# Attention: head pairs taken one by one, and taken by twos, on TensorE

## The chip, the cores and the metric

The kernel runs on one core of a Trainium2 chip. The core has five engines that run their own instruction streams and meet only at semaphores: TensorE (PE, matmuls; its weight loads are listed as PEld), VectorE (DVE), ScalarE (ACT), GpSimd (POOL) and SyncE (SP, which here only issues transfers). The metric is the device time of one execution in microseconds (us). Of the kernel before there are three timed runs, 787.14, 789.05 and 790.76 us, median 789.05.

## The reference, cut to what matters

Tokens `x` (8 sequences of 256 tokens, 256 wide) go through two layers: a mixture of experts twice, then attention and a third mixture of experts. Only the attention is touched by the change:

```python
xn = layernorm(x, g_in)
q = (xn @ Wq).reshape(b, n, H, DH).transpose(0, 2, 1, 3) * scale   # H = 16 heads of DH = 64
k, v = split(xn @ Wkv)                       # one key and one value head for all 16
k, v = concat([null_k, k]), concat([null_v, v])                    # one more key and value
sim = q @ k.T + bias ; sim = causal and padding masks applied
attn = softmax(sim)
out = (attn @ v) -> (b, n, H * DH) ; out = layernorm(out @ Wo, g_out)
```

## The kernel before, in words

**Units of work.** The 8 sequences are batches `b` = 0 to 7. The 16 heads of a batch are taken as 8 pairs, so there are 64 pairs `p = 8 b + j`. The two heads of a pair lie in partitions 0 to 63 and 64 to 127; the 256 queries are two tiles of 128 (`i`), the second of which sees all 256 keys and the null key, the first only 129 columns.

**The path of a pair.**
1. TensorE projects the queries (`pe_queries`, L1516, two fp32 matmuls of 256 columns, each of which runs as two instructions of the trace) into PSUM bank `psY`. ScalarE copies them, scaled, to `c_qr` (`act_queries`, L1764), a ring of two.
2. TensorE makes the scores (`pe_scores`, L1530, four matmuls on 64 rows of the array, two heads at a time) in `psH` or `psHT`.
3. VectorE adds bias and mask and takes the row minimum (`dve_scores`, L1907), once for each head (`ORDER[0]`, `ORDER[1]`). ScalarE takes the exponentials with their sums (`act_exp`, L1770).
4. VectorE turns the weights in 32x32 blocks (`dve_blocks`, L1932, once for each head), takes the reciprocals of the sums (`dve_sums`, L1914) and turns those too (`dve_recs`, L1921).
5. SyncE stores the pair's blocks (512 KB) in memory (`sp_store_blocks`, L2406) and loads them back in another order (`sp_load_blocks`, L2417). The turned blocks on chip (`c_x1`) are a ring of two: the blocks of pair p overwrite those of p - 2, so `dve_blocks` waits until the store of p - 2 has landed.
6. TensorE sums weights times values (`pe_sum`, L1543, four matmuls with 64 output partitions each) in PSUM bank `psL`. VectorE multiplies by the reciprocals into `c_oT` (`dve_o`, L1941). TensorE multiplies by the output weights and accumulates over the batch's pairs in `psM` (`pe_out`, L1554).

**The order by hand.** Each engine's stream is written out: at its step p, TensorE does scores(p + 1), sum(p - 4), queries(p + 3) and out(p - 5). VectorE does blocks(p, first head), scores(p + 1, first head), O(p - 4) (that is `dve_o`), blocks(p, second head), reciprocals(p), scores(p + 1, second head). Work that comes once per batch is placed at chosen steps j of the batch: on VectorE the row statistics of the next batch and part of the routing of an earlier one at j = 1, routing at j = 3, the batch's output, routing and output statistics at j = 5, routing at j = 7; on TensorE the turned rows, keys and values of the next batch (L1565, L1571, L1578) and three small pieces of routing (L1592, L1600, L1613). Each engine runs its stream in order, so an instruction that waits holds all that stand behind it on its engine.

## Time and profile before

| | |
|---|---|
| the profiled execution's own time | 789.7 us |
| its span | 788.0 us |
| TensorE busy | 706.1 us, 90% |
| VectorE busy | 453.5 us, 58% |
| ScalarE busy | 371.1 us, 47% |
| GpSimd busy | 431.0 us, 55% |
| mean TensorE clock granted | 0.954 |
| L1932 (blocks turned) idle before it, while a store lands | 10.0 us of 15.1 |
| L1516, L1554 (queries, outputs), each 256 instructions | 71.8 and 67.8 us |

The pairs' loop runs from about 375 to 645 us of the span. The shares above are means over stages with different limits; the loop is read from its own stretch. In a timeline row the columns are start, length, engine, line, operation, output and inputs, the count of instructions merged in the row, and in square brackets the idle time of the engine ahead of it with what ended it. A matmul's end is modelled, so of neighbouring matmuls the distance of their starts is the better measure. In a row of stretches the columns are start:end, length, then busy time and instruction count of PE, PEld, DVE, ACT and POOL, then the granted clock (1.00 is 2.4 GHz, 0.50 is 1.2 GHz), the busy share of the DMA engines and GB/s.

### The profile page before, as it was taken

The numbers are of one execution on the slowest core, as the hardware profiler recorded it, in microseconds if no ns is written. First come the engines' busy times: TensorE is split into PE (matmuls) and PEld (weight loads), VectorE is DVE, ScalarE is ACT, GpSimd is POOL, SyncE is SP. The second block draws the span as 40 slices with busy tenths as digits, with TensorE's granted clock in tenths as the row PEclk, the third lists the DMA queues.
The fourth block names the chain that finished last, engine by engine and source line by source line (L and its number), as shares of the span: only waits on it lengthen the run. The fifth ranks groups of instructions, "written<-read, shape, count | busy, mean of one in ns | idle before, by whom it ended". The sixth has DMA issues, their size and how long they took to land. (4 is left out here: it accounts for less than half of the span.)

```text
span 788.0 us, 15682 instructions
## 1 busy us (share of the span) xinstructions
PE 706.1 (90%) x4459; PEld 550.4 (70%) x4460; DVE 453.5 (58%) x1695; ACT 371.1 (47%) x1096; POOL 431.0 (55%) x540
## 2 busy tenths in 40 slices
PE   8859997875899999998799999899999998988886
PEld 5348984564799999986466666576666654787775
DVE  1803456358223322323988989799998945345546
ACT  3535641224222222223766766566766535666611
POOL 1175406541555575243876877898897645255550
PEclk9988999785899999999999999899999999999998
DMA  9734634332799877611899999887888883445428
GB/s 324 289 107 121 159 107 126 101 117 64 247 347 322 301 247 273 209 44 52 293 302 340 324 329 336 278 300 240 306 272 292 261 280 135 123 139 150 143 85 309
DMA packets 100571, 173.28 MB, mean 220 GB/s; under 512 B 11152, under 2 KB 73744, under 8 KB 99472
## 3 DMA queue, kind: packets, MB, share of 16 engines
q1 hardware_dynamic: 78064, 115.32, 43.5%
q0 software_dynamic: 10944, 30.03, 11.9%
q10 hardware_dynamic: 11488, 27.04, 10.3%
q8 instruction: 34, 0.56, 0.3%
q14 instruction: 41, 0.34, 0.1%
HBM read 111.73 MB, written 60.62 MB: 219 GB/s over the span
## 5 line engine op out<-in xcount | busy, mean ns | idle before, releaser
L1770 ACT ACTIVATE work<-work 128x129 f32<-128x129 f32 (+1 forms) x256 | 114.4, 448 | 76.1 <-DVE work L1907 74.5
L1932 DVE STREAM_TRANSPOSE region_bd<-work 128x384 f32<-128x384 f32 x128 | 73.2, 572 | 15.1 <-DMA c_blocks<-region_bd 10.0
L1409 POOL DMA_INDIRECT d_pairs<-work,home x47 | 48.1, 1022 | 51.5 <-DVE home_f L1161 36.4
L1516 PE MATMUL psY<-work,region_ac 128*128 128x256 f32 x256 | 71.8, 404 | 3.8 <-ACT work L1764 3.8
L2228 POOL TENSOR_TENSOR work<-region_bd,region_ac 128x386 f32<-128x386 f32 x64 | 59.7, 939 | 21.1 <-DVE work L1907 14.0
L2228 POOL TENSOR_TENSOR work<-work,region_ac 128x386 f32<-128x386 f32 x64 | 59.6, 943 | 20.8 <-DVE work L1907 15.0
L1398 POOL DMA_INDIRECT b_pairs<-work,home x39 | 38.0, 974 | 59.7 <-DVE work L1105 57.7
L1554 PE MATMUL psM<-region_ac,work 128*128 128x256 f32 x256 | 67.8, 388 | 0.0
L1390 POOL DMA_INDIRECT work<-in_x,inv x39 | 37.1, 951 | 53.8 <-DVE inv L1318 32.8
L1079 ACT ACTIVATE work<-work 128x512 f32<-128x512 f32 x39 | 24.6, 631 | 86.1 <-DVE work L1098 61.6
L1543 PE MATMUL psL<-region_bd,work 128*64 128x256 f32 (+1 forms) x512 | 56.4, 341 | 7.9 <-DMA region_bd<-c_blocks 4.1
L887 PE MATMUL psH<-work,region_bd 128*128 128x128 f32 x472 | 59.9, 282 | 3.0 <-issue 1.8
L887 PEld LDWEIGHTS psH<-work,region_bd 128*128 128x128 f32 x472 | 57.3, 198 | 4.0 <-issue 2.5
L1543 PEld LDWEIGHTS psL<-region_bd,work 128*64 128x64 f32 x512 | 32.0, 137 | 39.3 <-issue 23.1
L1468 POOL DMA_INDIRECT work<-a_slots,slot_u x32 | 31.5, 985 | 46.2 <-DMA a_slots<-work 27.3
L1516 PEld LDWEIGHTS psY<-work,region_ac 128*128 128x128 f32 x256 | 45.7, 194 | 14.5 <-ACT work L1764 5.8
L1390 POOL DMA_INDIRECT work<-y_scratch,inv x39 | 37.6, 965 | 33.1 <-DVE inv L1318 21.6
L1554 PEld LDWEIGHTS psM<-region_ac,work 128*128 128x128 f32 x256 | 47.7, 192 | 8.8 <-issue 2.8
L1770 ACT ACTIVATION_READ_ACCUMULATOR work<-work 128x1 f32 x256 | 47.9, 187 | 0.0
L1907 DVE CUSTOM_DVE_ANT_0 work<-psH,work 128x129 f32<-128x129 f32 (+1 forms) x128 | 39.6, 346 | 13.4 <-issue 10.9
L947 PE MATMUL psH<-work,region_bd 128*128 128x128 f32 x320 | 41.2, 285 | 0.0
L2309 POOL DMA_INDIRECT d_rows<-region_bd x32 | 32.2, 1005 | 15.7 <-issue 6.6
(390 smaller groups left out, 1614.0 us busy)
## 6 DMA issues: line engine op xcount, KB each, us to landing
c_blocks<-region_bd SPq DMA_DIRECT2D x64, 512.0 KB
region_bd<-c_blocks SPq DMA_DIRECT2D x64, 512.0 KB
region_bd<-in_b_w ACTq DMA_DIRECT2D x37, 512.0 KB
work<-d_rows SPq DMA_DIRECT2D x47, 132.0 KB
a_slots<-work SPq DMA_DIRECT2D x19, 256.0 KB
region_bd<-in_b_w SPq DMA_DIRECT2D x1, 4096.0 KB, 15.1
work<-b_pairs ACTq DMA_DIRECT2D x12, 256.0 KB
region_bd<-in_d_w SPq DMA_DIRECT2D x12, 256.0 KB
```

The source lines that it names most:

```text
L887: last = pe.matmul(pair_h[p % DEEP][:, t % PAIR, j, :], f.w_in(j, k, t), xT[:, p % DEEP, t % PAIR, k, :], start=(k == 0), stop=(k == KD - 1))
L947: last = pe.matmul(ffn_h[u % RING][:, j * P:(j + 1) * P], f.w_in(j, k, u % RING), b_xT[:, u % 2, k, :], start=(k == 0), stop=(k == KD - 1))
L1390: pool.indirect_dma_start(out=slot_rows(f, t), out_offset=None, in_=st.src, in_offset=bass.IndirectOffsetOnAxis(ap=inv[:, t:t + 1], axis=0 ...
L1398: pool.indirect_dma_start(out=st.pair_dram, out_offset=bass.IndirectOffsetOnAxis(ap=home[:, t:t + 1], axis=0), in_=ys[:, t % RING, :], in_ ...
L1409: pool.indirect_dma_start(out=st.pair_dram, out_offset=bass.IndirectOffsetOnAxis(ap=home[:, t:t + 1], axis=0), in_=d_ys[:, t % ROWS, :], i ...
L1516: last = pe.matmul(psY[:, 0:SEQ], c_wq[:, c, j * P:(j + 1) * P], c_xnT[:, odd, c, :], start=(c == 0), stop=(c == KD - 1))
L1543: last = pe.matmul(psL[DH * o:DH * o + DH, queries].rearrange("p (i a q) -> p i a q", a=4, q=32), c_v[:, b % 2, n, :], weights[:, o, block ...
L1554: last = pe.matmul(psM[:, i * DIM:(i + 1) * DIM], c_oT[:, p % 3, i * P:(i + 1) * P], c_wo[:, j, :], start=(j == 0 and i == 0), stop=(j == ...
L1770: nc.scalar.activation(c_p[:, j % 2, o, a:z], c_sc[:, o, a:z], ACT.Exp, scale=-1.0, bias=c_min[:, o, i:i + 1], accum_out=c_sum[:, j % 2, o ...
L1907: last = nc.vector.tensor_tensor_reduce(c_sc[:, o, a:z], psS[j % 2][:, o, a:z], c_bm[:, 2 * (j % 2) + o, a:z], 1.0, -LOWEST, ALU.add, ALU. ...
L1932: nc.vector.transpose(out=c_x1[:, p % 2, :, (QT + 1) * o:(QT + 1) * (o + 1), :].rearrange("p b i q -> p i b q"), in_=c_p[:, j % 2, o, 1:1 ...
L2228: pool.tensor_tensor(c_bm[:, 2 * (j % 2) + o, :], c_mp[b % 2], c_bias[:, 2 * j + o, :], ALU.subtract).then_inc(C.bm_ready, 1)
```

## The change

TensorE takes the pairs by twos. Its round for the even pair a is scores(a + 2) and scores(a + 3), sum(a - 4) and sum(a - 3), queries(a + 4) and queries(a + 5), out(a - 4) and out(a - 3). The queries of two pairs fill both halves of `psY`, and ScalarE copies both in one instruction, ahead of its exponentials at even steps. The sums of two pairs lie interleaved in `psL` (tile i, then pair, then 128 columns); one VectorE instruction of 512 columns multiplies both (`dve_o(p - 6)`, at even steps p, which does pairs p - 6 and p - 5). `c_oT` holds two pairs where it held three. On VectorE the reciprocals of an even pair move to the next, odd step, behind that step's first blocks, so their store is issued there. SyncE issues two stores, then two loads, then up to two weight loads. The small pieces of routing and of the next batch move to other places of TensorE's and ScalarE's streams.

```diff
 def pe_queries(pe, k, j, odd, b):
-            wait(pe, C.qr_ready, k)
+            wait(pe, C.qr_ready, k if k < 2 else k - k % 2)
-                last = pe.matmul(psY[:, 0:SEQ], c_wq[:, c, j * P:(j + 1) * P], c_xnT[:, odd, c, :],
+                last = pe.matmul(psY[:, (k % 2) * SEQ:(k % 2 + 1) * SEQ], c_wq[:, c, j * P:(j + 1) * P], c_xnT[:, odd, c, :],
...
 def pe_sum(pe, p, j, b):
-            wait(pe, C.o_ready, p)
+            wait(pe, C.o_ready, p - p % 2)
+            sums = psL[:, :].rearrange("p (i r a q) -> p i r a q", i=QT, r=2, q=32)[:, :, p % 2, :, :]
...
 def pe_batch(pe, b, odd, first, last):
+            for k in range(NPAIR // 2):
+                a = NPAIR * b + 2 * k
+                x = a - LAG
+                for p in (a + 2, a + 3):
+                    if p < pairs:
+                        pe_scores(pe, p, p % NPAIR, p // NPAIR)
+                for s in (x, x + 1):
+                    if s >= 0:
+                        pe_sum(pe, s, s % NPAIR, s // NPAIR)
+                if k == 0 and b >= 2:
+                    pe_z_turn(pe, b - 2)
+                if k == 1 and not first and not last:
+                    pe_rows(pe, b + 1)
...
+                if k == 3 and not last:
+                    pe_v_turn(pe, b + 1)
+                for p in (a + 4, a + 5):
+                    if p < pairs:
+                        pe_queries(pe, p, p % NPAIR, p // NPAIR % 2, p // NPAIR)
...
+                for s in (x, x + 1):
+                    if s >= 0:
+                        pe_out(pe, s, s % NPAIR, s // NPAIR)
...
+                if k == 0 and b >= 2:
+                    pe_route_bank(pe, a)
                     pe_z_logits(pe, b - 2, route_raw)
...
+                if k == 1 and not first and not last:
+                    pe_kv(pe, b + 1, 1 - odd)
+                if k == (1 if last else 3) and b >= 2:
+                    pe_route_bank(pe, a)
                     pe_z_counts(pe, b - 2, route_key)
...
+        def act_queries(act, k):
+            act.wait_ge(C.qr_mm, k + 2)
+            act.wait_ge(C.s_mm, k)
+            nc.scalar.mul(c_qr_both, psY[:, :], -(float(DH) ** -0.5)).then_inc(C.qr_ready, 2)
...
+        def dve_o(dve, p):
+            dve.wait_ge(C.pv_mm, p + 2)
             wait_dma(dve, C.blocks_loaded, 0, p)
+            wait_dma(dve, C.blocks_loaded, 0, p + 1)
+            wait(dve, C.wo_mm, p)
+            recs = c_x2_both[p // 2 % 2][:, :, :, 2 * (QT + 1):, :].rearrange("p r a i q -> p i (r a) q")
+            nc.vector.tensor_tensor(c_oT_both, psL[:, :].rearrange("p (i u q) -> p i u q", i=QT, q=32), recs, ALU.mult
+                                    ).then_inc(C.o_ready, 2)
...
 def dve_batch(dve, b, odd, first, last):
                 dve_blocks(dve, p, j, ORDER[0])
                 if j == 0 and not first:
                     dve_v(dve, b)
+                if j % 2 == 0 and p >= LAG + 2:
+                    dve_o(dve, p - LAG - 2)
+                if j % 2 == 1:
+                    dve_sums(dve, p - 1, j - 1)
+                    dve_recs(dve, p - 1)
                 if more:
                     dve_scores_wait(dve, p + 1)
                     dve_scores(dve, p + 1, j + 1, ORDER[0])
-                if s >= 0:
-                    dve_o(dve, s, s % NPAIR)
                 dve_blocks(dve, p, j, ORDER[1])
-                dve_sums(dve, p, j)
-                dve_recs(dve, p)
+                if j % 2 == 1:
+                    dve_sums(dve, p, j)
+                    dve_recs(dve, p)
```

TensorE before, one pair in the middle of a batch (here with the turned rows of the next batch, L1565, between queries and output):

```order
L1530 MATMUL psHT<-region_bd,work 128x129 [waits c_score_ready,c_qr_ready]
L1530 MATMUL psHT<-region_bd,work 128x129
L1530 MATMUL psHT<-region_bd,work 128x257 x2
L1543 MATMUL psL<-region_bd,work 64x256 [waits c_o_ready,c_v_ready,tokens_stored2]
L1543 MATMUL psL<-region_bd,work 64x256
L1543 MATMUL psL<-region_bd,work 64x128 x2
L1516 MATMUL psY<-work,region_ac 128x256 [waits c_qr_ready]
L1516 MATMUL psY<-work,region_ac 128x256
L1565 MATMUL psX<-ident,work 128x128 [waits d_tokT_ready,c_v_ready,c_xn_ready]
L1565 MATMUL psX<-ident,work 128x128 x3
L1554 MATMUL psM<-region_ac,work 128x256 [waits c_o_ready]
L1554 MATMUL psM<-region_ac,work 128x256
```

TensorE now, the round k = 2 of a batch and the first row of the next round (L1533 are scores, L1547 sums, L1519 queries, L1558 outputs):

```order
L1533 MATMUL psH<-region_bd,work 128x129 x2
L1533 MATMUL psH<-region_bd,work 128x257 x2
L1533 MATMUL psHT<-region_bd,work 128x129 x2
L1533 MATMUL psHT<-region_bd,work 128x257 x2
L1547 MATMUL psL<-region_bd,work 64x2x128 x2
L1547 MATMUL psL<-region_bd,work 64x128 x2
L1547 MATMUL psL<-region_bd,work 64x2x128 x2
L1547 MATMUL psL<-region_bd,work 64x128 x2
L1519 MATMUL psY<-work,region_ac 128x256 x4
L1558 MATMUL psM<-region_ac,work 128x256 x4
L1533 MATMUL psH<-region_bd,work 128x129 x2
```

Each kind of work now stands twice in a row. The end of that round again, with the semaphores that each row waits for (`c_o_ready` counts the pairs that VectorE's `dve_o` has done):

```order
L1519 MATMUL psY<-work,region_ac 128x256 [waits c_qr_ready,c_xnT_ready]
L1519 MATMUL psY<-work,region_ac 128x256
L1519 MATMUL psY<-work,region_ac 128x256 [waits c_qr_ready]
L1519 MATMUL psY<-work,region_ac 128x256
L1558 MATMUL psM<-region_ac,work 128x256 [waits c_out_raw,c_o_ready]
L1558 MATMUL psM<-region_ac,work 128x256
L1558 MATMUL psM<-region_ac,work 128x256 [waits c_o_ready]
L1558 MATMUL psM<-region_ac,work 128x256
L1533 MATMUL psH<-region_bd,work 128x129 [waits c_score_ready,c_kvT_ready,c_qr_ready]
```

The outputs here are of the pairs whose sums stand in the same round; before, the output at a step was of the pair whose sum stood one step earlier. VectorE before, one step up to the turned reciprocals:

```order
L1932 STREAM_TRANSPOSE region_bd<-work 128x3x4x32 [waits tokens_stored0,c_p_ready]
L1907 ISA work<-psHT,work 128x129 [waits c_p_ready,c_bm_ready,c_s_mm]
L1907 ISA work 128x1
L1907 ISA work<-psHT,work 128x257
L1907 ISA work 128x1
L1941 TENSOR_TENSOR work<-psL,region_bd 128x256 [waits c_wo_mm,tokens_stored2,c_pv_mm]
L1932 STREAM_TRANSPOSE region_bd<-work 128x3x4x32 [waits c_p_ready]
L1914 RECIPROCAL work<-work 128x4 [waits c_blocks_turned,c_p_ready]
L1921 STREAM_TRANSPOSE region_bd<-work 128x4x32 [waits c_rec_done]
L1921 STREAM_TRANSPOSE region_bd<-work 128x4x32
```

VectorE now, an even step and the first row of the odd step behind it (L1957 turns blocks, L1968 is `dve_o` for two pairs, L1932 are scores; `tokens_stored0` and `1` count the stores that have landed):

```order
L1957 STREAM_TRANSPOSE region_bd<-work 128x3x4x32 [waits tokens_stored0,c_p_ready]
L1968 TENSOR_TENSOR work<-psL,region_bd 128x512 [waits tokens_stored3,tokens_stored2,c_wo_mm,c_pv_mm]
L1932 ISA work<-psHT,work 128x129 [waits c_p_ready,c_bm_ready,c_s_mm]
L1932 ISA work 128x1
L1932 ISA work<-psHT,work 128x257
L1932 ISA work 128x1
L1957 STREAM_TRANSPOSE region_bd<-work 128x3x4x32 [waits c_p_ready]
L1932 ISA work<-psHT,work 128x129 [waits c_p_ready]
L1932 ISA work 128x1
L1932 ISA work<-psHT,work 128x257
L1932 ISA work 128x1
L1957 STREAM_TRANSPOSE region_bd<-work 128x3x4x32 [waits tokens_stored1,c_p_ready]
```

The multiplication now stands behind the first blocks of an even step, and this step has no reciprocals.

## Rows read from the trace of the kernel before

**Rows 1.** Stretches between stores: batches 1 and 2, 3, 4 to 6, 7.

```profile
402.80:469.38 66.58, 64.19 (x440) 44.47 (x438) 58.46 (x265) 44.77 (x167) 47.59 (x69) 1.00 0.97 330
469.38:506.43 37.05, 32.89 (x203) 23.11 (x200) 30.99 (x143) 22.77 (x84) 28.30 (x40) 0.91 0.90 313
506.43:605.74 99.31, 96.23 (x665) 67.83 (x665) 91.30 (x427) 67.91 (x252) 85.06 (x116) 1.00 0.83 279
605.74:633.56 27.82, 26.98 (x176) 17.15 (x173) 24.92 (x117) 15.79 (x59) 15.66 (x18) 1.00 0.85 279
```

**Rows 2.** Timeline of TensorE, late in batch 5.

```profile
563.04 1.03 PE L1516 MATMUL psY<-work,region_ac 128*128 128x256 f32 x4
563.91 1.03 PE L1554 MATMUL psM<-region_ac,work 128*128 128x256 f32 x4
...
568.71 0.93 PE L1530 MATMUL psHT<-region_bd,work 64*128 64x129 f32 x8
569.57 0.87 PE L1543 MATMUL psL<-region_bd,work 128*64 128x256 f32 x8
570.37 1.13 PE L1516 MATMUL psY<-work,region_ac 128*128 128x256 f32 x4
571.34 1.03 PE L1554 MATMUL psM<-region_ac,work 128*128 128x256 f32 x4
572.30 0.93 PE L1530 MATMUL psH<-region_bd,work 64*128 64x129 f32 x8
```

**Rows 3.** The same, two moments inside one pair's scores.

```profile
565.19 0.60 PE L1530 MATMUL psH<-region_bd,work 64*128 64x257 f32 x4
565.41 0.38 PE L1530 MATMUL psH<-region_bd,work 64*128 64x257 f32 x2
```

**Rows 4.** Timeline of TensorE, routing logits and the queries behind.

```profile
549.51 1.07 PE L1600 MATMUL psH<-d_gw,acc 128*128 128x16 f32 x8 [0.19 <-ACT acc L1792]
550.43 1.11 PE L1516 MATMUL psY<-work,region_ac 128*128 128x256 f32 x4
```

**Rows 5.** Timeline of VectorE, one plain step (j = 6) of batch 5.

```profile
563.55 0.57 DVE L1932 STREAM_TRANSPOSE region_bd<-work 128x384 f32<-128x384 f32 x1
564.57 0.41 DVE L1941 TENSOR_TENSOR work<-psL,region_bd 128x256 f32<-128x256 f32 x1
564.91 0.56 DVE L1932 STREAM_TRANSPOSE region_bd<-work 128x384 f32<-128x384 f32 x1
565.40 0.13 DVE L1914 RECIPROCAL work<-work 128x4 f32<-128x4 f32 x1
566.00 0.25 DVE L1907 CUSTOM_DVE_ANT_0 work<-psHT,work 128x129 f32<-128x129 f32 x1
566.53 0.57 DVE L1932 STREAM_TRANSPOSE region_bd<-work 128x384 f32<-128x384 f32 x1
```

**Rows 6.** VectorE, batch 5: around the work added at j = 1, 5, 7.

```profile
544.25 0.18 DVE L2027 TENSOR_TENSOR region_bd<-d_hot,psH 128x64 f32<-128x64 f16 x1
546.85 0.58 DVE L1932 STREAM_TRANSPOSE region_bd<-work 128x384 f32<-128x384 f32 x1
559.56 0.72 DVE L1950 TENSOR_TENSOR acc<-psM,work 128x256 f32<-128x256 f32 x2
568.98 0.15 DVE L2015 TENSOR_REDUCE region_bd<-psH 128x2 f32<-128x32 f32 x1
569.99 0.28 DVE L1907 CUSTOM_DVE_ANT_0 work<-psH,work 128x129 f32<-128x129 f32 x1
```

**Rows 7.** SyncE and VectorE: store of pair 47, and who waits for it.

```profile
569.09 0.32 SPq L2406 DMA_DIRECT2D c_blocks<-region_bd  x1
...
574.23 0.58 DVE L1932 STREAM_TRANSPOSE region_bd<-work 128x384 f32<-128x384 f32 x1 [0.41 <-DMA c_blocks<-region_bd]
```

**Rows 8.** TensorE in batch 3: its longest wait, and a stretch behind it.

```profile
497.07 1.55 PE L1543 MATMUL psL<-region_bd,work 128*64 128x256 f32 x8 [2.86 <-DMA region_bd<-c_blocks]
...
499.00:502.00 3.00, 3.00 (x8) 2.46 (x8) 2.87 (x16) 1.93 (x7) 1.52 (x2) 0.50 0.67 216
```

More of the change, by code:

```diff
@@ L1672, in pe_batch @@
-                if j == (1 if last else 2) and b >= 2:
-                    pe_z_turn(pe, b - 2)
-                if j == 3 and b >= 2 and not last:
-                    pe_z_logits(pe, b - 2, route_raw)
-                if j == 5 and last:
-                    pe_z_counts(pe, b - 2, route_key)
-                if j == 5 and not last:
-                    pe_kv(pe, b + 1, 1 - odd)
-                if j == 7 and not last:
-                    pe_v_turn(pe, b + 1)
-                over = (j + 3) // NPAIR
@@ L1683, in pe_batch @@
-                if not (last and over):
-                    pe_queries(pe, p + 3, (j + 3) % NPAIR, (odd + over) % 2, b + over)
-                if j == 1 and last:
-                    pe_z_logits(pe, b - 2, route_raw)
-                    pe_z_counts(pe, b - 3, route_key)
-                if j == 4 and not last:
-                    pe_rows(pe, b + 1)
-                if s >= 1 and j != 5:
-                    pe_out(pe, s - 1, (s - 1) % NPAIR, (s - 1) // NPAIR)
+                if k == 3 and last:
+                    pe_shared_halves(pe, 2, 3)
@@ L1835, in act_batch @@
                     act_load_pairs(act, b + 2)
-                if j == 5 and not last:
-                    act_keys(act, b + 1)
-                    act_values(act, b + 1)
                 if j == 7 and last:
@@ L2131, in dve_dispatch @@
                 dve_counted(dve, b - 3)
-            if j == (1 if last else 3) and b >= 2:
+            if j == 3 and b >= 2:
                 dve_key(dve, b - 2, route_raw, in_psum)
@@ L2198, in dve_attention @@
             batches(dve, dve_batch)
[L2199 to L2200 removed]
+            for j in range(NPAIR - LAG - 2, NPAIR, 2):
+                dve_o(dve, NPAIR * (BATCH - 1) + j)
             dve_out_raw(dve, BATCH - 1)
```

123 lines of the change are left out of this document (60 added, 63 removed).

## The prediction

> **What bounds the kernel now.** I read the page first, for where TensorE is full, then the busy times by stretch, then the timelines of TensorE and VectorE over one batch of the pairs' loop. The reader is to see three things. First, in the loop TensorE is busy nearly all the time: 96.2 of 99.3 us in batches 4 to 6, and VectorE is not far behind with 91.3 [rows 1]. Second, TensorE pays for each change of the kind of matmul. From start to start, scores, sum, queries and output of one pair take 0.86, 0.80, 0.97 and 0.96 us, together 3.59 [rows 2]. Queries that follow another 128-row, 128-column group take 0.87 instead of 0.97 [rows 2]: 0.10 us for a change at one end, and 0.10 at the other end of the output. Inside the scores a pass of 257 columns takes 0.22 us, both heads at once [rows 3]; two of these and two of half the width are 0.65 us, and the group takes 0.86. Third, VectorE's plain step is 2.98 us (563.55 to 566.53) [rows 5], while a batch takes 33.1 us, a third of 99.31: it has slack in plain steps, and none in steps with added work.
>
> **What the change takes off TensorE.** In a row, the second scores cost 0.65 and not 0.86, the second sum (the same columns, so also 0.65) 0.65 and not 0.80, and queries and outputs are 0.97 + 0.87 and 0.87 + 0.96. A round of two pairs is then 1.51 + 1.45 + 1.84 + 1.83 = 6.63 us, where two pairs took 7.18: 0.55 less, 17 to 18 us over 32 rounds, if TensorE set the pace alone.
>
> **What it takes off VectorE.** From the starts in rows 5: blocks and first scores 1.02 (0.49 + 0.53), multiplication 0.34, blocks 0.49, reciprocals 0.60, second scores 0.53. The multiplication of 512 columns is not in the trace; it costs between 0.34 and 0.68, and I take 0.65, since a pass over 384 columns in rows 5 takes 0.49 and the time follows the columns. So nearly nothing is saved. ScalarE's copy of 512 columns takes the place of two of 256; ScalarE is busy 67.9 of 99.3 us, and the copy stands ahead of the exponentials only when TensorE's queries are late. I cost it at nothing; at worst it delays one exponential per round by its own half microsecond.
>
> **What it adds: a wait in a ring.** Before, the output at a step needed a multiplication that VectorE had done a step earlier, with a sum and queries between. Now output(a - 4) stands in the round of its own sum and waits for the multiplication in VectorE's step a + 2. Behind the waiting output on TensorE stand the second output, then scores(a + 4), for which VectorE waits in step a + 3 before it can come to the next multiplication. That is a closed ring, and its length is a floor of the round:
> - TensorE: two outputs 1.83 + 0.10 (the weights of the first can't be loaded ahead) + scores until they are written, 0.93 [rows 2]: 2.86.
> - VectorE from the first scores of an odd step to the end of the multiplication: 0.53 + 0.49 + 0.60 + 0.53 + 0.49 + 0.65 = 3.29 [rows 5].
> - Two handovers of some 0.05 each: 6.25 us, under the 6.63 that TensorE needs anyway. But everything added on VectorE at odd steps, and everything that TensorE has between the outputs and the next scores, is now in the ring, one behind the other.
>
> On VectorE the added work is, each time less the 0.53 of the scores where they lie between: j = 1, 544.25 to 546.85, 2.07 us; j = 5, from 559.56 to 563.55 of rows 5, 3.46; j = 7, 1.01 [rows 5, 6]; at j = 3 four small operations like those of j = 7, at most 1.0. On TensorE behind the outputs: logits 0.92 at k = 0 [rows 4], keys and values at k = 1, which are four passes like the queries, 0.87.
>
> The round is (added behind the outputs) + the larger of 6.63 + (added on TensorE ahead of them) and 6.25 + (added on VectorE):
> - k = 0: 0.92 + 6.25 + 2.07 = 9.24.
> - k = 1: 0.87 + 7.1 (turned rows 0.45 ahead, half the queries' columns) = 7.97.
> - k = 2: 6.25 + 3.46 = 9.71. TensorE has 6.63 to do and sits idle for 3.1 in one piece.
> - k = 3: 6.25 + 1.01 + 0.3 for the values' copy and the counts = 7.56.
>
> A batch with all routing takes 34.5 us. Batches 4 to 6 took 33.1 each: 3 x 1.4 = +4.2. Batch 3 took 37.05, with a fall of the clock in it that need not come again: -2.6. In batch 1 (no routing) the same sum is 31.0, in batch 2 (no route counts) 33.9: 64.9 against 66.6, -1.7. For batch 7 and the end I add 1.5: one more output (0.96) and the longer multiplication stand behind the last sum. Batch 0 I leave. So far +1.4 us: the whole gain of TensorE is used up by the ring.
>
> **The stores.** The store of an even pair is now issued in the next, odd step, and blocks(a + 2) must wait until it has landed. Before, between the two lay the second scores and a whole step, 0.53 + 2.98 = 3.5 us at least. Now it is 0.53 + 0.49 + 0.60 + 0.53 = 2.15, plus what VectorE waits for TensorE (0.3 or more in the ring) and the step's added work. A store took 5.1 us before when VectorE had to wait for it (issued 569.09, landed 574.23) [rows 7]; without such a wait it took less. With 0.35 of such waiting, the work behind the outputs of the round before (0.14 of counts, 0.92, 0.87, 0) and the step's own (2.07, 1.0, 3.46, 1.01), the room is 4.7, 4.4, 6.8 and 3.5 us in the four rounds; against 5.1 that is 0.4, 0.7, 0 and 1.6 short at most. Two loads now go ahead of the store and are partly through by then, so I take 0.4 a batch in batches 3 to 6, 1.5 us in all, and 3.5 us in batches 1 and 2, where the DMA share is 0.97 [rows 1] and two weight loads are issued ahead of the store as well. Sum +5, between 0 and 14.
>
> **The clock.** In batch 3 TensorE sat idle for 2.86 us, and behind it the granted clock was 0.50, the 1.2 GHz level [rows 8]; over that batch 0.91 of 37.05 us [rows 1], 3.3 us lost. The idle piece of 3.1 us at k = 2 comes in five batches, 2 to 6. One such piece is all the trace has, so the price is between 0 and 5 x 3.3 = 16; I take two of the five, at 2.5, since part of a slow stretch falls in the wait: +5.
>
> **Sum.** Against the profiled execution's own 789.7 us (span 788.0): 1.4 + 5 + 5 = 11.4, so 801 us. The median of the timed runs, 789.05, lies 0.65 under the profiled one, which changes nothing here. About 0.5% (4 us) is what a measurement of this kernel can tell from no change.
>
> **A rule of the notes.** The sum's output in `psL` was one run of 256 columns and is now two runs of 128 with 128 columns between; no row of before shows such an output. The Trainium skill, "PSUM — Partial Sum Buffer", section "Specifications (TRN2)", gives lines of 8 bytes and says of an output pattern that is not contiguous that it slows matmuls significantly. It gives no figure, and its rule speaks against this change; it is rival D below.
>
> **Rivals.**
> A. Faster: the multiplication is done in time and TensorE or VectorE alone sets the pace. VectorE's two steps would be 5.93 us, 23.7 in a batch, with 7.5 added 31.2, against TensorE's 29.7. Then 33.1 becomes 31.2, seven batches give -13, and batch 3's lost clock -3: 773. For it: VectorE's slack in plain steps. Against it: the order, in which output(a - 4) can't pass before step a + 2. It needs an error in my reading of the ring. 0.15.
> B. The ring holds, but stores land in time and the clock stays: 789.7 + 1.4 = 791, from 786 to 794: no change to be seen. For it: stores may be quicker when less is asked of the DMA. 0.20.
> C. Slower by more: each of the five idle pieces costs the clock (+16 rather than 5) and the stores hold VectorE in most rounds without added work (+10): 817. For it: the one idle piece of this length did cost it. Decides where the idle piece is as long as computed and the store takes over 4 us. 0.17.
> D. The sums' first two matmuls run at half rate: two passes of 0.22 more per pair, 0.88 in TensorE's part of a round, which the wait at k = 0 and k = 2 hides, and k = 1 and k = 3 do not: 1.7 a batch, 13 in all, 815. 0.03.
> My forecast, the ring with some of both tolls, 794 to 808: 0.45.
>
> **How the numbers follow.** Faster by over 0.5% (under 785) is A and the low edge of B: 0.17. Within 0.5%: B's rest and 0.02 of the forecast, 0.19. Slower: 0.64. The range 784 to 817 leaves out A and the upper half of C and D. The likeliest case's own range is 794 to 808.
>
> **What would show it.** Right: TensorE's outputs wait for VectorE's multiplication in every round, longest at k = 2 with some 3 us; a batch of about 34 us in batches 4 to 6; between the second scores and their neighbour 0.65 us; VectorE's own waits for scores after the outputs, and waits for the stores at even steps above the 10 us of before. Wrong: rounds of 6.6 to 7 us without such waits (A); waits for stores that are gone or a clock at 1.00 throughout (B); sums of more than 0.8 us (D).

## The result, and the profile after

The kernel after takes 835.45 us, median of 6 runs (832.3 to 840.83), against 787.96 before (6 runs, 787.03 to 790.76): ratio 1.060, interval 1.056 to 1.064. It is slower, as forecast, but by 47 us and not by 12, and outside the range of 784 to 817.

The page's groups, kernel after (busy, mean ns of one, idle ahead of it and what ended most of that):

```profile
PE 708.7 (85%) x4459; PEld 565.1 (68%) x4460; DVE 453.2 (54%) x1663; ACT 370.8 (44%) x1065; POOL 431.8 (52%) x540
...
L1558 PE MATMUL psM<-region_ac,work 128*128 128x256 f32 x256 | 74.7, 442 | 48.4 <-DVE work L1968 48.4
...
L1957 DVE STREAM_TRANSPOSE region_bd<-work 128x384 f32<-128x384 f32 x128 | 73.7, 576 | 31.5 <-DMA c_blocks<-region_bd 25.9
```

L1558 is the output, L1968 the doubled multiplication, L1957 the blocks, L1533 and L1547 scores and sums, L2435 and L2446 store and load. No engine has much more to do (TensorE is busy for 708.7 us, before for 706.1). TensorE's outputs wait 48.4 us for the multiplication, where they waited for nothing before, and VectorE waits 25.9 us for stores, not 10.0.

Stretches of the kernel after that answer to [rows 1] (batches 1 and 2, batch 3, batches 4 to 6, batch 7 without its last step), and one that is read below:

```profile
412.01:496.43 84.42, 67.05 (x423) 49.66 (x421) 57.87 (x256) 44.92 (x159) 46.46 (x68) 0.88 0.75 260
496.43:537.59 41.16, 32.39 (x221) 24.39 (x221) 31.00 (x138) 22.86 (x80) 29.26 (x41) 0.92 0.80 279
537.59:647.36 109.77, 93.83 (x659) 71.23 (x659) 92.07 (x414) 67.92 (x240) 86.10 (x117) 0.97 0.72 255
647.36:683.00 35.64, 32.15 (x202) 21.79 (x201) 26.11 (x114) 16.17 (x56) 21.55 (x27) 0.95 0.76 272
522.89:529.72 6.83, 4.25 (x12) 3.06 (x14) 3.89 (x15) 1.98 (x8) 3.28 (x6) 0.50 0.71 253
```

Batches 1 and 2 took 66.58 and take 84.42 us; batches 4 to 6 took 99.31 and take 109.77 (forecast for the ring: 103.5). Nearly half of the loop's excess (17.8 of 38.6 us) lies in batches 1 and 2, where 13.5 of the 25.9 us of waits for stores are too. The DMA share there fell from 0.97 to 0.75: stores are late although the transfer engines are less busy. The waits of the loop (waiting engine and line, what ended it, us in total, times, longest), SyncE's own queue last:

```profile
PE psM L1558 <- DVE work L1968: 47.5, 25, 4.9
DVE work L1932 <- PE psH L1533: 27.0, 23, 3.9
DVE region_bd L1957 <- DMA c_blocks<-region_bd: 25.9, 13, 5.3
...
SPq L2435 <- DVE region_bd L1946: 115.1, 59, 5.2
SPq L452 <- DVE work L1968: 105.9, 29, 6.9
```

The last row is a wait that the prediction did not see: SyncE's loads wait for the multiplication (L452 is the wait for a free buffer), 105.9 us in 29 waits. SyncE works its stream in order, so a store that stands behind such a load could be held by it. The row above shows that this isn't what happens: 59 times the store itself, once SyncE had come to it, waited for its own turned reciprocals (L1946). In batches 1 to 7 every store of this trace but one is issued 0.03 us after them. What the bunched queue changes is how long a store takes to land; experiment 4 has the numbers.

One round of batch 3 on TensorE and VectorE shows how the two add up:

```profile
518.62 1.99 PE L1519 MATMUL psY<-work,region_ac 128*128 128x256 f32 x8
525.47 2.08 PE L1558 MATMUL psM<-region_ac,work 128*128 128x256 f32 x4 [4.85 <-DVE work L1968]
```

```profile
521.85 0.19 DVE L1990 TENSOR_SCALAR out_rstd<-out_mv 128x2 f32<-128x2 f32 x1
524.26 0.58 DVE L1957 STREAM_TRANSPOSE region_bd<-work 128x384 f32<-128x384 f32 x1 [2.22 <-DMA c_blocks<-region_bd]
524.76 0.65 DVE L1968 TENSOR_TENSOR work<-psL,region_bd 128x512 f32<-128x512 f32 x1
```

The multiplication stands behind the blocks, the blocks wait 2.22 us for a store, and TensorE's outputs, which the added work at j = 5 would have held up for some 2.6 us (4.85 - 2.22), wait 4.85. The clock is at 0.50, 1.2 GHz, from 522.89, inside this wait, to 529.72 (last row of the stretches above).

How to read the experiments: they ran on chips where the kernel before takes 747 to 749 us (only the last two on one where it takes 788). Chips differ outside the pairs' loop. The loop, from the first blocks to the last (372.3 to 632.9 and 375.7 to 674.9 in the profiles of before and after), takes 260.6 us on the one and 257.8 on the other kind before, and 299.2 and 299.8 after. So what is compared is the ratio to the kernel before on the same chip; loops and waits are of one execution each, which lay up to 9 us over its kernel's median (experiments 5 and 9) or 7 us under it (the queue in twos of experiment 4; 5 us in experiment 1, 4 in 6 and 8), so a difference of loops is no surer than that. The kernels before and after on such chips, whole loop:

```profile
343.40:601.20 257.80, 241.85 (x1634) 166.87 (x1633) 230.46 (x1070) 173.99 (x650) 202.32 (x276) 1.00 0.88 300
```

```profile
343.70:643.50 299.80, 244.74 (x1622) 182.34 (x1620) 231.52 (x1039) 173.19 (x619) 206.87 (x279) 0.94 0.73 256
```

> The kernel after, unchanged, on the chip of the other experiments, to have its loop and ratio beside theirs. Both theories: ratio 1.055 to 1.065, loop 297 to 303 us, waits for stores 24 to 30, clock loss in the loop 19 to 24 us. If its ratio were near 1.05 here, the filled kernel's 1.052 would be no gain at all.

Measured: ratio 1.059 (1.055 to 1.063), loop 299.8. The excess of the loop to be explained is 42 us.

### The profile page after: what moved, and what is told of

It reads as the page before. It is cut to its first block and busy times, and to the rows that moved or that the text cites. A ratio compares the mean times of both kernels' runs of the same rounds, so it can differ in the third digit from the quotient of the medians.

```text
span 836.0 us, 15599 instructions
## 1 busy us (share of the span) xinstructions
PE 708.7 (85%) x4459; PEld 565.1 (68%) x4460; DVE 453.2 (54%) x1663; ACT 370.8 (44%) x1065; POOL 431.8 (52%) x540
## 5 line engine op out<-in xcount | busy, mean ns | idle before, releaser
L1558 PE MATMUL psM<-region_ac,work 128*128 128x256 f32 x256 | 74.7, 442 | 48.4 <-DVE work L1968 48.4
L1558 PEld LDWEIGHTS psM<-region_ac,work 128*128 128x128 f32 x256 | 52.8, 216 | 68.5 <-DVE work L1968 60.1
L1957 DVE STREAM_TRANSPOSE region_bd<-work 128x384 f32<-128x384 f32 x128 | 73.7, 576 | 31.5 <-DMA c_blocks<-region_bd 25.9
L1519 PE MATMUL psY<-work,region_ac 128*128 128x256 f32 x256 | 65.2, 398 | 0.0
L1932 DVE CUSTOM_DVE_ANT_0 work<-psH,work 128x129 f32<-128x129 f32 (+1 forms) x128 | 40.1, 351 | 39.5 <-PE psH L1533 27.0
L1471 POOL DMA_INDIRECT work<-a_slots,slot_u x32 | 31.3, 977 | 48.2 <-DMA a_slots<-work 26.4
L1393 POOL DMA_INDIRECT work<-y_scratch,inv x39 | 37.7, 968 | 34.3 <-DVE inv L1321 21.5
L1519 PEld LDWEIGHTS psY<-work,region_ac 128*128 128x128 f32 x256 | 47.8, 196 | 8.8 <-issue 2.7
L1547 PE MATMUL psL<-region_bd,work 128*64 128x256 f32 (+1 forms) x512 | 49.4, 336 | 0.0
L1547 PEld LDWEIGHTS psL<-region_bd,work 128*64 128x64 f32 x512 | 32.2, 138 | 21.0 <-DMA region_bd<-c_blocks 6.0
L950 PE MATMUL psHT<-work,region_bd 128*128 128x128 f32 x304 | 37.9, 279 | 3.8 <-ACT work L1071 3.8
```

What stands on the lines that cost most here:

```text
L950: last = pe.matmul(ffn_h[u % RING][:, j * P:(j + 1) * P], f.w_in(j, k, u % RING), b_xT[:, u % 2, k, :], start=(k == 0), stop=(k == KD - 1))
L1393: pool.indirect_dma_start(out=slot_rows(f, t), out_offset=None, in_=st.src, in_offset=bass.IndirectOffsetOnAxis(ap=inv[:, t:t + 1], axis=0 ...
L1519: last = pe.matmul(psY[:, (k % 2) * SEQ:(k % 2 + 1) * SEQ], c_wq[:, c, j * P:(j + 1) * P], c_xnT[:, odd, c, :], start=(c == 0), stop=(c == ...
L1547: last = pe.matmul(sums[DH * o:DH * o + DH, queries, :, :], c_v[:, b % 2, n, :], weights[:, o, blocks, :, :], start=(n == 0), stop=(n == 1))
L1558: last = pe.matmul(psM[:, i * DIM:(i + 1) * DIM], c_oT[:, i, p % 2, :], c_wo[:, j, :], start=(j == 0 and i == 0), stop=(j == NPAIR - 1), s ...
L1932: last = nc.vector.tensor_tensor_reduce(c_sc[:, o, a:z], psS[j % 2][:, o, a:z], c_bm[:, 2 * (j % 2) + o, a:z], 1.0, -LOWEST, ALU.add, ALU. ...
```

## The experiments

**1. Reciprocals back in their own step** (kernel after otherwise).

```diff
-                if j % 2 == 1:
-                    dve_sums(dve, p - 1, j - 1)
-                    dve_recs(dve, p - 1)
...
-                if j % 2 == 1:
-                    dve_sums(dve, p, j)
-                    dve_recs(dve, p)
+                dve_sums(dve, p, j)
+                dve_recs(dve, p)
```

> The kernel after, but the reciprocals of the even pairs are back at the end of their own step, so that its store is issued some 1.6 us earlier; the doubled multiplication and the order on TensorE stay. Theory 1 (the stores were mis-sized: VectorE's 25.9 us of waiting for them, against 10.0 before, stand in the ring one behind the other with everything else, and the idle pieces they bring cost the clock too): the waits for stores fall to 10 us or less, the clock's loss of some 22 us falls by half, time 807 to 817. Rival (the ring alone is longer than computed and the stores only fill its waits): TensorE waits longer for the multiplication instead, time 828 to 836.

Measured: 1.062 (1.057 to 1.067), waits for stores 28.2 us, for the multiplication 47.8 (unchanged kernel 28.5 and 49.6). Theory 1 missed, and the rival's longer wait for the multiplication didn't come either: an earlier issue alone gains nothing. SyncE's timeline of this kernel:

```profile
565.06 0.92 SPq L2442 DMA_DIRECT2D region_bd<-c_blocks  x2
566.67 3.37 SPq L2431 DMA_DIRECT2D c_blocks<-region_bd  x2
574.87 0.92 SPq L2442 DMA_DIRECT2D region_bd<-c_blocks  x2
576.48 3.49 SPq L2431 DMA_DIRECT2D c_blocks<-region_bd  x2
```

The two loads are let go by the multiplication, and the store follows 1.61 us behind them, beside 1 MB of loads. Here the queue does hold some stores (8 of the even pairs' 28 in batches 1 to 7 are issued more than 0.3 us after their reciprocals, at most 1.2), but the landings eat the gain: the blocks that need an even pair's buffer now come 6.5 us after its store's issue instead of 5.6, but the store takes 5.9 us to land instead of 4.8 (medians, batches 1 to 7).

**2. Multiplication at the end of the odd step** (kernel after otherwise).

```diff
-                if j % 2 == 0 and p >= LAG + 2:
-                    dve_o(dve, p - LAG - 2)
...
                     dve_recs(dve, p)
+                if j % 2 == 1 and p > LAG:
+                    dve_o(dve, p - LAG - 1)
```

> The kernel after, but the doubled multiplication of pairs (a-4, a-3) is done at the end of the odd step a+1, ahead of the added work, and not in step a+2. The ring then is outputs 1.93 + scores 0.93 + first scores 0.53 + blocks 0.49 + reciprocals 0.60 + multiplication 0.65 = 5.1 us with no added work in it. Theory 1 (ring): TensorE's 48.4 us of waiting for the multiplication fall under 15, and the time by 20 to 30 us to 806 to 816, with the waits for stores (26 us) left or a little longer. Rival 2 (stores lead): the wait moves from the multiplication to the stores, time 825 or more. Rival 3 (the strided output or the paired order itself is slow): no change, 833 or more.

Measured: 1.028 (1.025 to 1.032), loop 278.0. The outputs' waits for the multiplication fall from 49.6 to under 1 us, those for stores stay at 27.8. Half of the excess goes with the ring opened, as theory 1 said. A new wait of 23.1 us comes in its place: TensorE's second scores (L1533) wait for VectorE's (L1932).

**3. Both.**

> Both edits: reciprocals in their own step and the multiplication at the end of the odd step. Theory 1: no ring, no late stores, the clock as before or better; TensorE's round 6.63 and VectorE's 5.93 plus 7.5 of added work in a batch give some 31.5 to 32 us a batch against 33.1 before: 770 to 782, faster than the kernel before. Rival (pairing loses even without ring and stores, because work in twos makes both engines wait for each other): 790 to 800.

Measured: 1.039 (1.036 to 1.042), slower than edit 2 alone. Its waits in the loop:

```profile
DVE work L1968 <- issue: 26.4, 28, 2.4
PE psHT L1533 <- DVE work L1932: 25.9, 20, 3.6
DVE region_bd L1957 <- DMA c_blocks<-region_bd: 19.7, 11, 5.1
```

VectorE now comes to the multiplication before the sums are written and waits there; the second scores stand behind it, and TensorE's scores(a + 3) wait for those: a second ring. It is in experiment 2 too (8.9 us for the multiplication, 23.1 for the scores). The view names no releaser for the first row, but the longest of these waits can be followed: it ends with the multiplication's start at 563.12, and TensorE's sums, under the slow clock there, run from 560.18 for 2.83 us, to 563.01:

```profile
560.18 2.83 PE L1547 MATMUL psL<-region_bd,work 128*64 128x256 f32 x16
```

```profile
563.12 0.69 DVE L1968 TENSOR_TENSOR work<-psL,region_bd 128x512 f32<-128x512 f32 x1 [2.43 <-issue]
```

**4. The kernel before with late reciprocals alone, and with SyncE's queue in twos alone.** The first moves the even pairs' reciprocals to the odd step, the second is

```diff
-            for p in range(pairs):
-                sp_store_blocks(sp, p)
-                if p >= 1:
-                    sp_load_blocks(sp, p - 1)
...
+            for a in range(0, pairs, 2):
+                for p in (a, a + 1):
+                    sp_store_blocks(sp, p)
+                for p in (a, a + 1):
+                    sp_load_blocks(sp, p)
```

> The kernel before (pairs one by one on TensorE), with one thing of the change alone: the reciprocals of even pairs are made in the next step, ahead of its first scores, so the store of an even pair is issued later by about 1.6 us less the work between. Theory 1a (the store's delay by itself costs what the change's waits show): waits for stores 20 us or more, time 797 to 805. Theory 1b (the forecast's own term, +5, holds without the ring): 791 to 796. Rival (only the order of SyncE's queue, two stores and then two loads, makes the stores late): 787 to 790.

> The kernel before with SyncE's order alone taken from the change: two stores, two loads, two weight loads. Load(a+1) now stands ahead of store(a+2) and waits for the landing of store(a+1). Theory (the queue in twos is one of two causes of the late stores, the late reciprocals with 3.1% are the other): ratio 1.01 to 1.025, waits for stores 18 to 28 us. Rival (order of the queue is harmless without the ring, where loads wait for a late multiplication): 0.997 to 1.008.

Measured: late reciprocals 1.031 (1.027 to 1.034), waits for stores 35.4 us; queue in twos 1.041 (1.036 to 1.046), waits for stores 36.2. Both cost more than expected (theory 1a's 797 to 805 of 788 us is 1.011 to 1.022). The four runs of the queue in twos spread widely, from 768.9 to 782.4 us; by the medians (776.17 against 747.63) it is 1.038. SyncE's waits in the loop, kernel before, and with the queue in twos:

```profile
SPq L2417 <- DMA c_blocks<-region_bd: 22.4, 18, 2.9
```

```profile
SPq L2417 <- DMA c_blocks<-region_bd: 114.4, 60, 5.6
SPq L2406 <- DVE region_bd L1921: 100.5, 50, 3.5
```

The loop with the queue in twos:

```profile
342.00:623.90 281.90, 251.03 (x1635) 172.46 (x1635) 229.41 (x1070) 173.98 (x651) 204.64 (x278) 0.96 0.81 273
```

Load(a + 1) has to wait until store(a + 1), issued just ahead of it, has landed. The Trainium skill ("DMA: Bandwidth & Descriptors", section "Anatomy of one DMA — SWDGE (gpsimd) path") says, of transfers that GpSimd issues, that DMA engines don't wait on semaphores, and that the wait is spent on the issuing sequencer ahead of the dispatch. The rows agree for SyncE's transfers: the wait shows on SP, and the DMA share falls from 0.88 to 0.81.

Store(a + 2) stands behind that load, but it is seldom held by it: 50 times SyncE still had to wait for the store's own reciprocals (second row), and only 2 of the 28 even pairs' stores of batches 1 to 7 are issued more than 0.3 us after them. The cost is in the landing. The semaphore updates in the traces give the time from an even pair's issue to its store's landing (batches 1 to 7, the 23 to 28 stores of which all updates are recorded, medians), and the waits for stores:

| kernel | issue to landing, us | of these, batches 1 and 2 | waits for stores in the loop |
|---|---|---|---|
| before | 3.7 | 4.5 | 12.2 |
| before, late reciprocals | 3.0 | 3.1 | 35.4 |
| before, queue in twos | 5.7 | 7.6 | 36.2 |
| before, both (experiment 9) | 4.3 | 6.5 | 32.9 |
| after | 4.8 | 6.0 | 28.5 |
| after, reciprocals in their own step (1) | 5.9 | 6.9 | 28.2 |
| after, queue as before (5) | 3.1 | 3.3 | 24.2 |

So there are two ways to a late store. Late reciprocals leave it less room before its buffer is needed; the queue in twos makes it land later. The likely reason is the two loads that are then issued just ahead of it (1.61 us in experiment 1), whose transfers run beside its own; with both edits it is issued later, when more of the loads is through, and lands sooner than with the queue alone. No run separates this reason from others.

**5. SyncE's queue as before** in the kernel after, and in the kernel of experiment 2.

> The kernel after with one thing undone: SyncE issues store(p), load(p-1) and one weight load in turn, as before, and not two stores, two loads, two weight loads. Multiplication and reciprocals stay as changed. Theory 1 (transfers in bunches make the stores late: the first experiment issued them earlier and gained nothing because they then ran beside two loads): waits for stores fall from 26 to 15 us or less, mostly in batches 1 and 2, the loop from 299 to 285 to 290, ratio to before 1.042 to 1.05. Rival (the bunches don't matter, the late issue does): ratio 1.057 to 1.064.

> Multiplication at the end of the odd step (which gave 1.028) and SyncE's queue alternating as before; the reciprocals of even pairs stay in the odd step. Theory 1: the two gains add, loop 278 to 265 to 269, ratio 1.005 to 1.018. Rival (late reciprocals alone hold the stores, as the 1.031 of the kernel before with them shows): waits for stores stay at 25 us or more and the ratio at 1.025 to 1.03.

Measured: 1.037 (1.032 to 1.042) and 1.035 (1.031 to 1.038). Undoing the queue's order takes 2 points off the change, with the waits for stores only down from 28.5 to 24.2 and those for the multiplication from 49.6 to 38.6. Beside the early multiplication it gains nothing (1.028 without it, on another chip), as the rival said: with late reciprocals 36.5 us of waits for stores remain, as the 35.4 of experiment 4.

**6. Transfers cut to 32 of 128 rows** (stale data beyond them, so hardly a store or load of the loop is late), after and before.

> The kernel after, with the stores and loads of the blocks cut to 32 of 128 rows from pair 4 on (the rest of the data is stale), so that no transfer is late; beside it the kernel before with the same cut. Theory: waits for stores fall under 3 us in both, and what is left of the difference is the ring and the clock: the loop is longer than the cut kernel before's by 15 to 25 us. Forecast as written (ring +1.4, clock +5): 6 us. Rival (all of the excess comes from late transfers): under 4 us.

> The kernel before, with the same cut of the stores and loads to 32 of 128 rows from pair 4 on (stale data beyond them). It has 12 us of waits for stores and 2 of waits for loads in the loop; with these gone the loop takes 244 to 252 us against 258: ratio 0.968 to 0.99.

Measured: 1.021 (1.015 to 1.027) and 0.992 (0.988 to 0.995); waits for stores 5.5 and 0.7 us. The loops, after and before:

```profile
341.20:612.30 271.10, 235.72 (x1622) 177.06 (x1620) 231.54 (x1039) 172.44 (x619) 205.60 (x279) 0.97 0.41 117
```

```profile
342.40:595.90 253.50, 241.71 (x1634) 167.22 (x1633) 231.46 (x1070) 173.59 (x650) 204.26 (x278) 1.00 0.44 126
```

So ring and clock make 17.6 us of loop without late transfers. Whole transfers add 28.7 us (299.8 - 271.1) to the kernel after and 4.3 (257.8 - 253.5) to the one before: 24.4 us of the 42 need transfers of full size. By the medians of the timed runs ring and clock make 21.5 us (762.73 - 741.24) of 44 (0.059 x 748), which leaves 22. Most of that is lost in batches 1 and 2, where weights are loaded as well: with cut transfers these take 66.5 us (374.21 to 440.75, clock 1.00), as in the kernel before (66.6), and with whole ones 82.5 (84.4 on the first chip). Batches 4 to 6 take 109.4 with cut transfers and 110.8 with whole ones (109.8 on the first chip): there the excess is ring and clock almost alone. The three of the kernel after with cut transfers:

```profile
473.29:511.42 38.13, 33.66 (x222) 25.48 (x221) 30.58 (x139) 22.49 (x80) 29.08 (x41) 0.91 0.31 85
511.42:546.37 34.95, 30.17 (x221) 23.10 (x220) 30.70 (x141) 22.63 (x80) 29.12 (x41) 1.00 0.33 92
546.37:582.69 36.32, 31.68 (x220) 24.07 (x219) 30.58 (x141) 22.62 (x80) 27.47 (x38) 0.95 0.28 74
```

At full clock a batch takes 34.95, where 34.5 was forecast. The batches at 0.95 and 0.91 lose 1.8 and 3.4 us to the clock (0.05 x 36.32, 0.09 x 38.13) and are 1.4 and 3.2 longer. That fits a us of time for a us of clock, but it is two batches set beside one, and not an experiment on the clock.

**7. All but the pairs undone**: reciprocals in their own step, the queue as before, multiplication behind the second scores of the odd step. Two variants: in step 5 the multiplication ahead of the routing work; and sums ahead of the scores on TensorE.

```diff
                 if more:
                     dve_scores(dve, p + 1, j + 1, ORDER[1])
+                if j % 2 == 1 and p > LAG:
+                    dve_o(dve, p - LAG - 1)
```

> Reciprocals in their own step, SyncE's queue alternating as before, and the multiplication at the end of the odd step behind the second scores, not ahead of them. With both earlier edits VectorE waited 26 us for the sums ahead of the multiplication, 0.8 in each odd step, and TensorE's scores(a+3) waited 26 us for the second scores that stood behind it: a second ring. Theory 1: that wait falls under 5 us and the stores' under 10, loop 252 to 260, ratio 0.985 to 1.0. Rival (work in twos loses in itself): ratio 1.01 or more.

> The version at 1.004 (reciprocals in their own step, SyncE's queue alternating, multiplication behind the second scores of odd steps), but in step 5, where VectorE has 2 to 3 us of routing work ahead of those scores, the multiplication stands ahead of that work. Theory: the outputs' waits for it (9.7 us) fall under 4 and the slow stretches behind them go with it: ratio 0.99 to 1.0, a little faster than both kernels at best. Rival (TensorE's scores wait for the second scores instead, now 0.65 later): 1.003 to 1.01.

> Reciprocals in their own step, SyncE's queue alternating, multiplication at the end of the odd step ahead of the routing work and the second scores, and on TensorE the two sums ahead of the two scores of a round, so that the multiplication finds them written. The ring is outputs 1.93 + sums 1.45 + scores 0.93 + 2.27 on VectorE = 6.6, as long as TensorE's own round. Theory: neither wait of the versions at 1.004 (9.7 for the multiplication, 13 for the second scores) is left above 5 us: ratio 0.985 to 1.0. Rival (the sums now delay the first scores and VectorE waits for them): 1.005 to 1.02.

Measured: 1.004 (1.001 to 1.007), its first variant 1.004 (1.001 to 1.007), its second 1.008 (1.005 to 1.010). No version in twos beats the kernel before. Loop of the first:

```profile
341.90:605.90 264.00, 235.48 (x1628) 175.69 (x1628) 229.48 (x1039) 172.30 (x620) 206.43 (x281) 0.97 0.86 292
```

The pairs do save TensorE 6.4 us of matmuls (235.48 against 241.85), and it is idle 28.5 us where it was idle 16.0. VectorE's 230 us didn't shrink. The wait of 26.4 us of experiment 3 is 1.2 here, and TensorE's for the second scores 13.6 where it was 25.9. How much of this is the multiplication's place is not shown: the queue was changed together with it, and in experiment 5 the queue alone, beside the early multiplication, took the wait for the second scores from 23.1 to 12.9. Of the new waits 9.7 us for the multiplication and the 13.6 are left; those for stores are 12.7, as before. So the last half per cent is not shown to be a price of the pairs as such.

**8. Filling the idle piece.** TensorE turns the unit matrix in the third round of batches 1 to 6 while it waits, 10 or 24 times, in the kernel after.

```diff
+                if k == 2 and not first and not last:
+                    pe.wait_ge(C.kvT_ready, 3 * (b + 1) + 3)
+                    for _ in range(24):
+                        pe.transpose(psX[:, 0:P], ident[:, :], ident[:, :])
                 for s in (x, x + 1):
```

> The kernel after, with 10 turns of the unit matrix (some 0.27 us each) on TensorE in the third round of batches 1 to 6, between the queries and the outputs, where it waits 2.5 to 4.9 us for the multiplication; their result is not read. Clock theory: the slow stretches behind these pieces (6.8 us each in batches 2 and 3, 3.4 in 4 and 6) go, the granted clock of batches 2 to 6 is above 0.95, and of the 10 us that they cost 5 to 10 come back: ratio to before 1.048 to 1.055. Rival (the clock falls and the ring's waits hide it): the clock rises and the ratio stays at 1.058 to 1.064; if the clock doesn't change either, idle pieces are not what lowers it.

> As the filled kernel, but 24 turns and not 10: ten took only 1.25 us in a row and covered a quarter to a half of the idle piece; 24 take 3.0. Clock theory: in batches 2, 3, 4 and 6 no slow stretch follows the third round, and the loop is 3 to 8 us shorter than the unfilled one's on the same chip; where the wait for the multiplication was under 3.0 us the filler costs up to 0.5 us a batch. Rival: the clock rises and the loop doesn't shorten, since waits take the room.

Measured: 10 turns 1.052 (1.046 to 1.058), 24 turns 1.063 (1.059 to 1.067), unfilled 1.059 (on the chip of the 24 turns; the 10 ran on another). With 24, which take 2.78 us, no slow stretch of the clock begins in the 9 us behind a filled piece; over the loop the clock is 0.95, not 0.94 (the slow stretches sum to 27.3 us instead of 37.5, 5 us of lost clock less), and the loop 298.3 us, not 299.8. That fits idle pieces that bring slow stretches, but what filling them is worth is inconclusive: the two fillings lie on both sides of the unfilled kernel, the filler has a price of its own where the wait was shorter than it, and the two longest slow stretches (6.83 us, both in batch 1) lie elsewhere.

**9. The ring alone and the store edits alone**: the kernel after with reciprocals and queue undone, and the kernel before with both of these edits.

> The kernel after with both things that act on the stores undone (reciprocals in their own step, SyncE's queue alternating), and the doubled multiplication left in the even step: the ring by itself, with whole transfers. Theory 1 (ring and late stores are separate costs; with transfers cut to a quarter the ring was worth 17.8 us of loop, 8.5 of them lost clock): waits for stores 8 to 14 us, loop 272 to 280, ratio 1.018 to 1.03. Forecast as written for the ring alone (+1.4): ratio 1.002 or, with its clock term, 1.008. Rival (in the ring every wait for a store goes straight to TensorE, so even few cost much): 1.035 or more.

> The kernel before with both edits that make stores late, and nothing else of the change: reciprocals of even pairs in the odd step (alone 3.1%) and SyncE's queue in twos (alone 4.1%); TensorE's order, the single copies and the single multiplications stay. Theory 1 (they are two ways to the same lateness, so they overlap): waits for stores 36 to 50 us, ratio 1.04 to 1.055. Rival (they add): 1.07 or more. If the ratio is at or over the 1.059 of the whole change, the paired order on TensorE with its ring costs nothing in their presence.

Measured: 1.021 (1.018 to 1.025), loop 284.2, waits for stores 15.5 us; and 1.020 (1.015 to 1.025), loop 274.2, waits for stores 32.9 (in kernel before 10.0). The ring alone is 2.1%, the store edits alone 2.0%, and the whole 5.9 to 6.0%. By these medians 1.8 points, some 14 us, exist only where both are there; by the loops, whose execution of the ring alone lay 9 us over its median, it is 1.4 us (38.6 less 23.6 and 13.6). And the single edits give no surplus: the ring (2.1%) and the queue in twos alone (3.8 to 4.1%) sum to 5.9 to 6.2%, and with both of them, but reciprocals in their own step, experiment 1 measured 6.2%; late reciprocals on top of that add nothing. So ring and queue, simply added, also give the whole, and that the two multiply is not shown.

That both store edits together cost less than either alone (3.1 and 4.1%) was not expected. Part of it the landings of experiment 4 explain (4.3 us with both, 5.7 with the queue alone); that it is also under the late reciprocals alone stays open, and these were measured on different chips.

## Why the prediction was wrong

**TensorE's own gain: right.** Two sums take 1.45 us from start to start (593.66 to 595.11 below), two scores 1.51, as computed. Rival D (a slow split output) is refuted, and for this shape the rule of the Trainium skill that it stands beside ("PSUM — Partial Sum Buffer", section "Specifications (TRN2)"): the outputs of two runs of 128 columns cost no more than one run of 256. TensorE in batch 5, the kernel after:

```profile
573.96 0.93 PE L1533 MATMUL psH<-region_bd,work 64*128 64x129 f32 x8
581.38 1.99 PE L1558 MATMUL psM<-region_ac,work 128*128 128x256 f32 x8 [2.08 <-DVE work L1968]
...
584.10 0.93 PE L1533 MATMUL psH<-region_bd,work 64*128 64x129 f32 x8
...
592.15 0.93 PE L1533 MATMUL psH<-region_bd,work 64*128 64x129 f32 x8
592.91 0.82 PE L1533 MATMUL psHT<-region_bd,work 64*128 64x129 f32 x8
593.66 1.52 PE L1547 MATMUL psL<-region_bd,work 128*64 128x256 f32 x16
595.11 1.99 PE L1519 MATMUL psY<-work,region_ac 128*128 128x256 f32 x8
599.88 1.99 PE L1558 MATMUL psM<-region_ac,work 128*128 128x256 f32 x8 [2.77 <-DVE work L1968]
601.80 0.93 PE L1533 MATMUL psH<-region_bd,work 64*128 64x129 f32 x8
...
611.22 0.93 PE L1533 MATMUL psH<-region_bd,work 64*128 64x129 f32 x8
```

**The ring: right in mechanism and place, right in size for a plain batch, too small over the whole.** Rounds of batch 5 were forecast at 9.24, 7.97, 9.71 and 7.56 us; the starts of their scores (573.96, 584.10, 592.15, 601.80, 611.22) give 10.14, 8.05, 9.65 and 9.42, the last with a wait of 1.90 for a store inside. (By its own rule of the larger the second is 0.87 + 7.25 = 8.12, and not 7.97.) Without late transfers a batch at full clock takes 34.95 against 34.5. Over the whole, though, +1.4 was too little: the ring alone measured 2.1%, 17 us. That is the ring with the clock that it loses (0.95 over the loop) and the few late stores of the kernel before; ring and clock terms together were forecast at +6.4. The term was made small by 4.3 us that batches 1 to 3 of before lost to clock and transfers and "need not" lose again; they lost more. And it was a sum at full clock, while the ring keeps making the idle pieces behind which the clock falls.

**The stores: this step failed.** The term was +5, between 0 and 14. Late transfers are worth 22 to 24 us (experiment 6), and taking both store edits out of the whole change gives back 30 (47.5 less 17.4, experiment 9). Of this, 16 to 18 us lie in batches 1 and 2, for which 3.5 were forecast; in batches 4 to 6 the forecast 0.4 a batch was about right (110.8 us with whole transfers, 109.4 with cut ones). Three things in the term were wrong. It took the moved issue as the only cause, while the queue's new order by itself costs about 4% and lets the store land after 5.7 us instead of 3.7 (experiment 4), in batches 1 and 2 after 7.6: I wrote that the two loads now ahead of the store "are partly through by then", and no row stood behind that. It took a store's time as fixed at 5.1 us and reckoned the room on VectorE alone; with the reciprocals moved back the room grew by 0.9 us, the landing by 1.1, and the ratio did not fall (1.062, experiment 1). And it added the stores to the ring, while a late store is in the ring: the blocks that wait for it stand ahead of the multiplication (2.22 of the 4.85 us in batch 3). Whether this makes the two cost more than their sum is not settled (experiment 9: 14 us more by one set of numbers, nothing by another).

**The clock: the place right in part, the size nearly four times too small, its share not settled.** Forecast was +5 from two of five idle pieces. The loop of after has the clock at 0.94, before's at 1.00 (second kind of chip): 0.06 x 300 = 18 us lost. The forecast counted idle pieces of 3 us at k = 2 of batches 2 to 6. With late stores they are up to 4.9 us long and come at other rounds and in batch 1 as well, and batches 1 and 2 alone, at 0.88, lost 0.12 x 84.42 = 10 us. How much of the time that clock costs stays open: in the ring without late transfers two batches fit a us for a us (experiment 6); in the whole kernel filling the idle piece brought no time that can be told (experiment 8).

**Rivals.** A (multiplication in time) is refuted by the 48.4 us, B (ring only) gave 791 and would have been 1.021, 805 us, C (817) had the right two mechanisms and was still 18 us short: it gave late stores 10 us where experiments 6 and 9 give them 22 to 30.

## What to carry to other kernels

When transfers are bunched, ask what runs beside each one, and not only when it is issued: here the order of one queue, with the same transfers, moved a store's landing from 3.7 to 5.7 us. Read the issuing engine's waits before you blame its queue: a row that names the store's own input says that the loads ahead did not hold it. A wait that stands in a closed ring has to be followed once round before it is priced. Work in twos saves changes of the kind of matmul on one engine and doubles the grain at which the others are let go; in the best version here what was saved and what was lost came out nearly even (1.004), with some 23 us of new waits still in it.

## What the runs showed of the hardware

In the pairs' loop the granted clock's slow stretches came in lengths of 3.41 and 6.83 us in every trace, always at 0.50. A store of 512 KB took 3.0 to 5.9 us to land (medians) by what was queued beside it. Ten turns of the unit matrix (128 x 128) in a row took 1.25 us, where a turn of that shape has a record of 0.27: a record's length is no price of a matmul in a row. The same program took 788 us in two comparisons and 747 to 749 on four other chips; the executions differ by 29 us ahead of the loop (it starts at 372.3 and at 343.4) and by 12 behind it (155.1 and 143.2 us), and in the loop by 3. The cause was not looked into.
